# A recurrent layer's prologue: constants loaded one stage earlier, convolution ahead of the step sizes, half of the decay tables made inside the units

## The reference, cut to what matters

```
x = x + 0.5 * experts8(layernorm(x))
x = x + mixer(layernorm(x))          # the recurrent layer
x = x + 0.5 * experts8(layernorm(x))

mixer(h):
  gate, xBC, dt = split(h @ in_proj_w.T)        # 512, 768, 64 columns
  xBC = silu(causal_conv4(xBC) + conv_b)        # x: 512, B: 128, C: 128
  dt  = clip(softplus(dt + dt_bias), 0, 100)
  a   = -exp(A_log) * dt                        # 64 heads of 8 channels
  state_t = exp(a_t) * state_(t-1) + B_t (x_t * dt_t)
  y_t = C_t . state_t + D * x_t
  y   = rmsnorm(y * silu(gate)) * norm_w
  return y @ out_proj_w.T
```

## Time and profile before

| | us |
|---|---|
| median of 3 runs (1039.57 to 1041.65) | 1039.83 |
| the profiled execution's own time | 1041.49 |
| its span, first to last instruction | 1039.5 |
| PE busy in the span | 857.8 |
| DVE busy | 596.7 |
| POOL busy | 492.4 |
| ACT busy | 396.5 |
| mean granted TensorE clock (share of full speed) | 0.934 |

### The profile page before, as it was taken

The page is one execution under the profiler, slowest core; times in us unless marked ns, Lnnn a source line. Parts: engine busy times, 40 slices in busy tenths (PEclk is TensorE's granted clock), DMA queues, the critical chain, the costliest instruction groups (busy, mean ns, idle before and its releaser), DMA issues.

```text
span 1039.5 us, 21523 instructions
## 1 busy us (share of the span) xinstructions
PE 857.8 (83%) x7798; PEld 556.2 (54%) x7799; DVE 596.7 (57%) x1105; ACT 396.5 (38%) x955; POOL 492.4 (47%) x538
## 2 busy tenths in 40 slices
PE   3099976787778679998589999969689978999995
PEld 2046642332323335664389999633434444799994
DVE  5623336688796242334535655648389845655655
ACT  6322223145557242224234444356401125344441
POOL 2228868048888331213235454223588733455531
PEclk9999988998978889998879999999899988999997
DMA  8313443235656810002946665330000001766644
GB/s 293 108 42 113 124 128 121 108 94 184 187 174 213 320 59 14 31 21 88 412 163 244 240 221 203 97 137 1 0 0 1 1 1 45 275 221 244 244 167 137
DMA packets 47752, 142.25 MB, mean 137 GB/s; under 512 B 10577, under 2 KB 23714, under 8 KB 41154
## 3 DMA queue, kind: packets, MB, share of 16 engines
q0 software_dynamic: 19280, 93.40, 26.7%
q1 hardware_dynamic: 22366, 40.92, 11.0%
q10 hardware_dynamic: 6036, 6.95, 2.0%
HBM read 106.11 MB, written 35.16 MB: 136 GB/s over the span
## 4 chain that ended last, share of the span: by engine, by line
PE 51%; POOL 13%; DMA 12%; DVE 11%; issue 7%; ACT 5%; SPq 1%; POOLq 0%; ACTq 0%; DVEq 0%
PE psum L563 15%; PE psum L536 12%; PE psum L522 8%; PE psum L1826 4%; POOL mem L1538 4%; POOL mem L1536 3%; DMA mem<-w2l_dram 2%; DMA stage<-in_w 2%; POOL mem L246 2%; PE psum L509 1%; PE psum L1853 1%; PE psum L114 1%; DVE mem L1449 1%; DVE mem L315 1%; DVE psum L2033 1%
## 5 line engine op out<-in xcount | busy, mean ns | idle before, releaser
L563 PE MATMUL psum<-mem 128*128 x1536 | 178.9, 273 | 3.7 <-DVE mem L801 2.5
L563 PEld LDWEIGHTS psum<-mem 128*128 128x128 f16 x1536 | 146.3, 98 | 23.9 <-issue 4.7
L912 POOL DMA_INDIRECT y_dram<-mem x64 | 63.4, 991 | 150.4 <-DVE mem L817 147.6
L536 PE MATMUL psum<-mem 128*128 128x128 f16 x2208 | 132.4, 220 | 0.0
L536 PEld LDWEIGHTS psum<-mem 128*128 128x128 f16 x2208 | 128.6, 99 | 0.7
L653 ACT ACTIVATE mem<-psum,mem 128x128 f32<-128x128 f32 x368 | 105.1, 369 | 55.1 <-PE psum L536 53.6
L907 POOL DMA_INDIRECT mem<-xn_dram,mem x64 | 65.8, 1029 | 113.8 <-PE psum L509 85.9
L1403 ACT ACTIVATE mem<-psum 128x512 f32<-128x512 f32 (+1 forms) x160 | 79.9, 552 | 77.0 <-PE psum L1299 50.8
L522 PE MATMUL psum<-mem 128*128 x432 | 102.7, 397 | 0.7 <-issue 0.7
L1449 DVE TENSOR_REDUCE mem<-psum 128x2 f32<-128x1024 f32 (+2 forms) x96 | 87.6, 949 | 20.4 <-PE psum L1273 12.2
L114 PE MATMUL psum<-ones 128*128 128x512 f16 x326 | 92.3, 413 | 0.6 <-issue 0.6
(11 more groups left out here) (250 smaller groups left out, 1481.9 us busy)
## 6 DMA issues: line engine op xcount, KB each, us to landing
stage<-in_w POOLq DMA_DIRECT2D x20, 480.0 KB, 5.1
stage<-in_w POOLq DMA_DIRECT2D x16, 512.0 KB, 3.9
w_rows<-mem SPq DMA_DIRECT2D x4, 2048.0 KB, 21.0
w2h_dram<-mem POOLq DMA_DIRECT2D x20, 240.0 KB, 2.9
w2l_dram<-mem POOLq DMA_DIRECT2D x20, 240.0 KB, 4.4
xn_dram<-mem ACTq DMA_DIRECT2D x32, 128.0 KB, 1.7
mem<-w2h_dram SPq DMA_DIRECT2D x2, 2048.0 KB, 13.2
mem<-w2l_dram SPq DMA_DIRECT2D x2, 2048.0 KB, 19.1
```

The lines of the kernel that those rows point to most:

```text
L536: ins = eng.matmul(c.bank(2 * p + j // half)[:, j % half * P:(j % half + 1) * P], mats[q][:, l, k, j * P:(j + 1) * P], x[:, p, k, :], star ...
L563: ins = eng.matmul(c.bank(6)[:, 0:D], a[:, 0 if gated else p, q * half + j, :], w[:, at], start=(i == 0), stop=(i == 3 * CF - 1))
L912: eng.indirect_dma_start(c.y_dram[:, :], bass.IndirectOffsetOnAxis(ap=yidx[:, b:b + 1], axis=0), yo[:, b % 2, :], None).then_inc(s_ys[b % ...
```

## The change

It does four things. The twelve loads move from `sync` to `prefetch`, which SP runs ahead of the eight-expert stage's own part; it waits for the first half of the first block's first product (`begun`) instead of for the last tile of x. The small tables (`vec`, `conv`, `norm`, and `re`) and `gmask` get other places in `mem1`, behind the slabs. The mixer's `sync` keeps a wait on `s_c` and issues nothing. The first group's convolution goes ahead of the step sizes on DVE, and its tap between Exp and Ln on ACT. Eight of the sixteen tables stay in the prologue: four behind the fourth channel group, four behind the fifth. The other eight are made in the first four units, two ahead of each: PE makes them, ACT takes their Exp behind its last copy of xt, and POOL multiplies four of them by dt at the places of units 0 to 3. B's transposes wait only for B's silu, and the silus and copies on ACT are put in another order.

```diff
 TABLES = [("end", LEVELS), ("all", 0)] + [(m, k) for k in range(LEVELS - 1, -1, -1) for m in ("base", "end")]
-TABLE_STEPS = (0, 0, 3, 4, 4, 5)
+TABLES_FIRST = 8
...
-    def sync(eng):
+    def prefetch(eng):
         for w in after:
             eng.wait_ge(*w)
-        eng.wait_ge(*src["done"](src["count"]))
+        eng.wait_ge(*src["begun"])
...
+    def sync(eng):
+        eng.wait_ge(*s_c(16 * 6))
...
# PE, prologue
+        for i in range(4):
+            channels(i)
+        for j in range(TABLES_FIRST // 2):
             table(eng, j)
+        channels(4)
+        for j in range(TABLES_FIRST // 2, TABLES_FIRST):
+            table(eng, j)
+        channels(5)
...
+        eng.wait_ge(*s_si(1))
+        turned(0, bb)
         eng.wait_ge(*s_si(2))
-        turned(0, bb)
...
# PE, units
         for i, (p, k) in enumerate(UNITS):
+            for j in range(TABLES_FIRST + 2 * i, min(TABLES_FIRST + 2 * i + 2, len(TABLES))):
+                table(eng, j)
...
# in table(eng, j)
+        if TABLES_FIRST <= j < TABLES_FIRST + 2:
+            eng.wait_ge(*s_tc(10))
+        elif j >= 2:
             eng.wait_ge(*s_te(j - 1))
...
# ACT
+        eng.wait_ge(*s_dn(1))
+        eng.activation(e, e, ACT.Exp).then_inc(s_de.sem, 1)
+        tap(0)
+        eng.wait_ge(*s_de(1))
+        eng.activation(e, e, ACT.Ln, bias=1.0).then_inc(s_dl.sem, 1)
+        tap(1)
+        tap(2)
...
         turned(4)
+        for j in range(TABLES_FIRST, len(TABLES)):
+            decay(j)
...
# DVE
         eng.scalar_tensor_tensor(e, r, -1.0, r, ALU.mult, ALU.min).then_inc(s_dn.sem, 1)
+        convolve(0)
         eng.wait_ge(*s_dl(1))
...
-        for i in range(NX):
+        for i in range(1, NX):
             convolve(i)
...
# DVE, base(i)
-            if i == 0:
-                eng.wait_ge(*s_te(len(TABLES)))
+            eng.wait_ge(*s_te(TABLES.index(("base", k)) + 1))
...
# POOL
+            for j in range(TABLES_FIRST + 2 * i, min(TABLES_FIRST + 2 * i + 2, len(TABLES))):
+                weigh(j)
...
# program(): stages
+            if n + 1 < len(stages) and stages[n + 1] == "s":
...
+                progs.append(dict(sync=mixer["prefetch"]))
             progs.append(st)
```

More of the change, by code:

```diff
@@ L942, in moe_stage @@
     return dict(pe=pe, act=act, dve=dve, pool=pool, sync=sync, done=s_xd, count=NT, order=list(range(NT)),
-                ready=lambda i: s_xd(i + 1), combine=[combine_first, combine_second][:TOPK], idle_bank=3, idle_before=28 if gated else 14)
+                ready=lambda i: s_xd(i + 1), combine=[combine_first, combine_second][:TOPK], begun=s_h1(1), idle_bank=3, idle_before=28 if gated else 14)
 def l1_weights(c, A, stage, w1_split, w2_stored, w1_h, w1_l, w2_h, w2_l, rr_h, rr_l, rw2, cb, region, after, slabs):
@@ L1609, in level_units, with mixer_stage @@
     return out
-def mixer_stage(c, src, A, region, region2, stage, after):
+def mixer_stage(c, src, A, region, region2, stage, after, loads_at):
     n = lambda name, total: c.sem("mix_" + name, total)
@@ L1637, in mixer_stage @@
     region2.at = at + 4 * 4 * T
+    assert region2.at >= loads_at
     bb = take2([T], F32)
@@ L1641, in mixer_stage @@
     masks = take2([len(TABLES), P], F32)
+    vec = take2([3, NH], F32)
+    conv = take2([NX, CONV_K + 1], F32)
+    norm = take2([INTER // P], F32)
+    re = take2([2, NT, NH], F32)
     dt = take2([NT, NH], F32)
     a = take2([NT, NH], F32)
[L1644 to L1647, removed]
     gl = take2([NT], F32)
@@ L1664, in mixer_stage @@
     region2.at = max(end, region2.at)
+    gmask = take2([LEVELS, P], F32)
     flat = stage[:, :, :].rearrange("p a b -> p (a b)")
@@ L1761, in pe, with channels @@
         ins.then_inc(s_dp.sem, 1)
[L1762 to L1766, removed]
+        def channels(i):
             if i >= 3:
@@ L1772, in pe @@
                     for w, x in three((wx_h, wx_l), xT):
-                        ins = eng.matmul(c.bank(2 * (i % 3) + q), w[:, k, ch * P:(ch + 1) * P], x[:, k, q * BANK:(q + 1) * BANK],
-                                         start=(m == 0), stop=(m == 3 * KD - 1))
+                        ins = eng.matmul(c.bank(2 * (i % 3) + q), w[:, k, CHANNELS[i] * P:(CHANNELS[i] + 1) * P],
+                                         x[:, k, q * BANK:(q + 1) * BANK], start=(m == 0), stop=(m == 3 * KD - 1))
                         m += 1
             ins.then_inc(s_xc.sem, 1)
-        while j < len(TABLES):
+        for i in range(4):
+            channels(i)
+        for j in range(TABLES_FIRST // 2):
             table(eng, j)
-            j += 1
+        channels(4)
+        for j in range(TABLES_FIRST // 2, TABLES_FIRST):
+            table(eng, j)
+        channels(5)
         def turned(i, src):
@@ L1787, in turned @@
                 else:
-                    eng.wait_ge(*s_te(len(TABLES) - 1 + g))
+                    eng.wait_ge(*s_te(TABLES_FIRST - 1 + g))
                 for b in range(4):
@@ L1885, in act @@
         eng.activation(vec[:, 1, :], vec[:, 1, :], ACT.Exp).then_inc(s_al.sem, 1)
[L1886 to L1889, removed]
         def dest(i):
@@ L1915, in turned @@
                 eng.activation(dst, src, ACT.Copy).then_inc(s_tc.sem, 1)
-        j = 0
-        for i in range(NX):
[L1919 to L1923, removed]
-            decay(j)
-            j += 1
+        eng.wait_ge(*s_dn(1))
[5 more added lines that the diff above has]
+        tap(2)
+        for j in range(TABLES_FIRST // 2):
+            decay(j)
+            if j == 1:
+                tap(3)
+        for j in range(TABLES_FIRST // 2, TABLES_FIRST):
+            decay(j)
+            if j == TABLES_FIRST // 2 + 1:
+                tap(4)
         silu(0)
+        tap(5)
         silu(1)
+        turned(0)
         silu(2)
-        turned(0)
+        silu(3)
+        turned(1)
         eng.wait_ge(*s_gp(1))
@@ L2085, in pool, with weigh @@
         eng.wait_ge(*s_a(1))
-        for j, (m, k) in enumerate(TABLES):
+        def weigh(j):
+            m, k = TABLES[j]
             if m == "end":
@@ L2089, in pool @@
                 eng.tensor_tensor(wl[:, k, :, :], wl[:, k, :, :], dt[:, :, :], ALU.mult).then_inc(s_wl.sem, 1)
+        for j in range(TABLES_FIRST):
+            weigh(j)
         eng.wait_ge(*s_ge(2))
@@ L2134, in pool @@
                 todo[what](t)
-    return dict(pe=pe, act=act, dve=dve, pool=pool, sync=sync, done=s_xd, count=NT,
+    return dict(prefetch=prefetch, pe=pe, act=act, dve=dve, pool=pool, sync=sync, done=s_xd, count=NT,
                 order=list(range(NT)), ready=lambda i: s_xd(i + 1), combine=[], idle_bank=4)
@@ L2296, in program @@
             elif kind == "s":
+                st = mixer
+            if n + 1 < len(stages) and stages[n + 1] == "s":
                 reg = Region(mem0, size0)
                 reg.at = mixer_at
-                st = mixer_stage(c, st, A, reg, Region(mem1, 4 * E1 * KD * FF), stage, [split1["done"](split1["count"])])
+                mixer = mixer_stage(c, st, A, reg, Region(mem1, 4 * E1 * KD * FF), stage, [split1["done"](split1["count"])],
+                                    4 * SLABS * SLAB)
+                progs.append(dict(sync=mixer["prefetch"]))
             progs.append(st)
```

5 lines of the change are left out of this document (1 added, 4 removed).

## The result

The changed kernel takes 1029.26 us (median of 4 runs, 1028.34 to 1030.51) against 1040.45 us for the kernel before (4 runs, one more than in the table of before), a ratio of 0.9888 with a 95% interval of 0.987 to 0.9905. The forecast was 1024.0 with 1019.5 to 1031 around it: the time lies in the range, but of the forecast gain of 16 us 11 came. The profiled execution took 1029.48 us, its span is 1027.9 (before: 1041.49 and 1039.5).

What follows compares the result with a forecast made beforehand. The prediction saw a gapless 58.35 us prologue path, then units paced by PE, `base` on DVE, PE. Prologue -19.2, units +2.95, loads +0.3 gave -15.95: 1039.83 to 1023.9, about 1024 us, range 1019.5 to 1031.

Steps and rivals of the forecast that it cites:

- The start of the prologue: Step sizes: PE starts at about 685.25 instead of 687.62, 48 matmuls take 1.6 us, tables begin 3.8 us earlier.
- ACT sets the rest: Late prologue: ACT's table load, silus, taps and copies set the pace, G's copies ending at 718.1 and six copies at 723.4.
- `wd` ends last: End of prologue: `wd` ends at 724.3, after ACT's 723.4; DVE's first unit instruction comes 19.2 us earlier.
- I take the full clock: PE's products for G in the prologue: full clock after waits of 1.1 us or less; low clock makes G 1.2 later.
- The loads' new place: Expert blocks: loads take 8.2 us, fourth block's rows just meet their deadline, later blocks have room; cost 0.3, bounds 0 and 3.
- rival A: Expert blocks: the loads make the rows of a block or two 3 us late, 1027 us; chance 0.12.
- The units: First four units: eight tables made there cost 2.95 us, bounds 0.5 and 7.2; unit 0 moves by 0.5.
- its wait covers the difference: Units: POOL, 4.8 late while PE is 2.95 late, has a 1.54 us wait for DVE that absorbs the difference.
- the stretching of DVE: Units: POOL instructions can hold DVE up to 1.07 us each, 4.3 in all; taken as 0, with 4.3 in the range.
- B: New prologue: PE falls to the low clock, costing about 3.5 us, 1027.5 us; chance 0.12.
- C: Prologue: only the early tables and shorter list count, gain 8.4 us, 1031.4 us; chance 0.10.
- D: Units: tables become a serial chain of 4.84 us per unit, slower than before, 1041.6 us; chance 0.04.

Runs made afterwards that it cites:

- e5: Changed kernel with the twelve loads back behind the last tile of x, new order kept: 1034.27 us, 0.9922 of the kernel before.
- e7: Changed kernel with the first convolution back behind the step sizes on DVE and its tap behind Ln on ACT: 1029.77 us, 0.9891 of the kernel before.
- e9: Changed kernel with the loads' trigger at block 20 and tables 8 and 9 ahead of PE's first B product: 1024.25 us, 0.9841 of the kernel before.
- e10: Changed kernel with loads' trigger at block 20, tables 8 and 9 ahead of the first B product, seven idle matmuls before G's products: 1022.91 us, 0.9826.
- e8: Changed kernel with POOL's four multiplications by dt in the units cut to 2 of 64 columns: 1026.64 us, 0.9854 of the kernel before.
- e3: Changed kernel with tables 8 and 9 ahead of PE's first B product: 1027.18 us, 0.988 of the kernel before.
- e1: The changed kernel run again without further edits: 1029.03 us, 0.9888 of the kernel before.
- e4: Changed kernel with the loads' trigger at block 19 and tables 8 and 9 ahead of the first B product: 1027.09 us, 0.9859 of the kernel before.

## Why the prediction came out as it did

*The start of the prologue: right.* PE began at 686.95, 0.15 us behind the layer norm, the 48 matmuls took 1.4 us (1.6 forecast, at a granted clock of 1.00; with the wait back in e5, 2.62 us of it, the granted clock was down again, 0.68 over the first 2.5 us), and the tables began 12.15 us behind the layer norm for 12.2 forecast. That the convolution in front holds back `a` and yet costs nothing was checked by e7.

*ACT sets the rest, `wd` ends last: right.* 39.1 us were forecast for the prologue; it took 38.4 with the clock up and 39.8 with it down, so at the clock that I had assumed the sum of the pieces was 0.8 too long, and it hides half of what the clock cost. The step "I take the full clock" was a coin toss: a wait of 0.94 us was followed by either. The price of 1.2 for the low clock was 1.46.

*The loads' new place: the mechanism of rival A, and my sum for it was wrong.* I tested the fourth block's rows, which did come in time, and then wrote that every later block has more room because the loads are gone by 546. That took the full 427 GB/s for the loads, while two lines before I had given half of it to the gathers: with the other half the loads need 16.5 us, until 549, and the last landed at 552.3. The fifth block's rows are issued behind that block's own 1.05 MB of weights, at 537.82, when all twelve loads had been issued. The term was +2.7, with 0.3 taken and 3 as its bound. With the loads behind the blocks (e5) no block waits; a trigger at block 19 wins back about half, one at block 20, behind the last gathers, leaves no wait (e9, e10).

*The units: 2.95 forecast, 4.9 paid.* What failed was unit 0: I put the two tables in the gap before the second `cs`, and did not carry on to the first `bx` what I had read in the earlier trace rows for other places, that PE ran at the lower level behind waits of 2.69 and 4.0 us. Unit 0 came 2.0 late where 0.5 was forecast, and about 1.8 of it is the clock. On POOL I wrote that its wait covers the difference, and I put the stretching of DVE at 0; e8 says that 0.8 us get through, by that stretching. Without the low clock unit 8 would stand some 3.1 us late (e3, with two tables fewer in the path: 2.8), near the 2.95, but partly by luck: I had all of it in place at unit 3, where e3 lost only 1.9, and the 0.8 that I had put at nothing filled the rest.

*Rivals B to D.* B, the low clock, came true in part, at the two places named. C fell: the gain in the prologue was 18.5 and not 3.8 plus tables. D fell: no instruction in the units waited for a multiplication made in the same unit.

*The sum.* For the profiled execution 1025.5 was forecast and 1029.48 measured, 4.0 more: 2.4 from the loads' stretch, 0.7 from the prologue, 0.7 from the units (where 2.1 more were paid and 1.4 came back by the clock at the output), 0.6 from the two untouched stretches, less 0.4 outside the span. The other 1.4 of the 5.4 us between the forecast median and the measured one is no mechanism: I had taken the profiled execution of before to stand 1.66 above the median, and that of after stands 0.22 above.

## What to carry to other kernels

A load that is moved "under" another stage takes its share of the DMA engines from that stage's gathers: test every gather until the load has landed, not the first, count the same share of the engines in every line of the sum, and put the trigger where the last gathers have been issued. Where work is moved so that an engine waits, ask what clock TensorE has behind the wait, and fill the wait with work that is due anyway. Order in a prologue by what frees the next resource (here PSUM banks), not by what the longest chain needs first.

## What the runs showed of the hardware that I had not expected

Behind the same wait of 0.94 us, at the same place of the same program, TensorE's granted clock was 1.00 in one run (e1, 16 records in 2.05 us) and 0.54 in another (3.56 us). Even behind a wait of 2.44 us, late in the layer, 4 records took 1.95 us in e5 and e8 and 3.56 in e4. Before a difference of 1 or 2 us between two profiles is put down to an edit, these places have to be held against each other. And a 128 KB gather that lands early enough in quiet blocks took 9.87 us when 1.05 MB on its own queue and 3.52 MB on another had been asked for ahead of it.
